# A four-layer convolution kernel: the order of work in the offset stage, the index arithmetic in halves, layer 1's projection by quarters

## The reference

```
om = conv3x3(x, offset_w) + offset_b            # 27 values per position: 18 offsets, 9 masks
dy, dx, mask = om[0:18:2], om[1:18:2], sigmoid(om[18:27])
py, px = row + tap_row + dy, column + tap_column + dx
y0, x0 = floor(py), floor(px);  ly, lx = py - y0, px - x0
val = bilinear(x at (y0, x0), (y0, x0+1), (y0+1, x0), (y0+1, x0+1); ly, lx) * mask
out = relu(batch_norm(einsum(val, weight) + bias))
```

## Time and profile before

| | |
|---|---|
| median of 3 runs | 4148.88 us (4147.64 to 4153.2) |
| profiled execution | 4145.01 us, its span 4143.2 us |
| mean granted clock of TensorE | 0.905 of full |
| busy share of the span | PE 82%, DVE 78%, POOL 54%, PEld 52%, ACT 48% |
| offset stages start (first L838 of the last group norm) | 795.0, 1760.9, 3692.9 us in samples 0, 1 and 3 |

### The profile page before, as it was taken

The page is one execution under the profiler, slowest core; times in us unless marked ns, Lnnn a source line. Parts: engine busy times, 40 slices in busy tenths (PEclk is TensorE's granted clock), DMA queues, the critical chain, the costliest instruction groups (busy, mean ns, idle before and its releaser), DMA issues.

```text
span 4143.2 us, 79222 instructions
## 1 busy us (share of the span) xinstructions
PE 3416.2 (82%) x28785; PEld 2163.6 (52%) x28785; DVE 3239.3 (78%) x6687; ACT 1972.0 (48%) x4413; POOL 2234.6 (54%) x2476
## 2 busy tenths in 40 slices
PE   4999868879999966979999976979999976982555
PEld 2666623447777732336777742435777752342444
DVE  5999767489999856669999956749999966745666
ACT  2444332446666622346666742345666653242333
POOL 3454450068878641038878824018887845005775
PEclk9999989989999988979999988989999998995555
DMA  1000101155555402055555512045555520117775
GB/s 49 9 12 12 42 7 44 60 165 148 154 151 156 120 19 49 14 160 154 150 151 151 153 40 48 2 127 143 156 152 152 151 80 22 39 46 213 219 220 176
DMA packets 219934, 426.57 MB, mean 103 GB/s; under 512 B 27825, under 2 KB 126540, under 8 KB 217512
## 3 DMA queue, kind: packets, MB, share of 16 engines
q0 software_dynamic: 92160, 302.06, 25.3%
q1 hardware_dynamic: 127346, 119.53, 10.0%
q10 hardware_dynamic: 54, 0.01, 0.0%
HBM read 340.77 MB, written 60.65 MB: 97 GB/s over the span
## 4 chain that ended last, share of the span: by engine, by line
PE 37%; DVE 29%; issue 12%; POOL 10%; POOLq 4%; DVEq 3%; ACT 2%; SPq 2%; DMA 1%; ACTq 0%
DVE val L1233 9%; PE bank L548 7%; DVE mxc L1196 7%; PE bank L688 6%; DVE xl L1256 5%; POOL G L1595 3%; DVE val L1243 3%; PE bank L732 3%; PE bank L716 2%; POOLq L1570 2%; PE bank L749 2%; PE bank L475 2%; POOL reg L1595 1%; POOL x_cur L1595 1%; PE bank L571 1%
## 5 line engine op out<-in xcount | busy, mean ns | idle before, releaser
L1606 POOL TENSOR_TENSOR xl<-pt 128x192 bf16<-128x192 f32 (+1 forms) x1024 | 685.5, 670 | 422.6 <-PE bank L548 206.4
L868 ACT ACTIVATE pt<-bank 128x512 f32<-128x512 f32 x1024 | 608.2, 594 | 573.9 <-PE bank L517 343.0
L1595 POOL DMA_INDIRECT G<-patch_table,idx x576 | 593.9, 1031 | 191.9 <-issue 115.1
L548 PEld LDWEIGHTS bank<-vt,pt 128*128 128x128 bf16 x8192 | 548.5, 98 | 242.1 <-ACT pt L868 3.9
L548 PE MATMUL bank<-vt,pt 128*128 128x129 bf16 (+1 forms) x8192 | 632.7, 220 | 1.1 <-ACT osb L876 1.1
L1196 DVE TENSOR_REDUCE mxc<-bank 128x1 f32<-128x512 f32 x896 | 607.1, 679 | 29.0 <-PE bank L475 27.3
L1256 DVE TENSOR_TENSOR xl<-pt 128x320 bf16<-128x320 f32 (+1 forms) x1024 | 504.2, 493 | 72.8 <-PE bank L548 53.7
L548 PE MATMUL bank<-vt,xl 128*128 128x129 bf16 x4096 | 401.2, 221 | 12.8 <-DVE xl L1256 12.7
L1580 POOL TENSOR_TENSOR rs<-ve,mhalf 128x4 f32<-128x4 f32 x32 | 34.9, 1092 | 619.6 <-ACT ve L995 619.6
L475 PE MATMUL bank<-reg,qh 128*128 128x512 bf16 x896 | 341.4, 382 | 13.6 <-DVE mxc L1196 10.1
L688 PE MATMUL bank<-reg,val 128*32 128x512 bf16 x3264 | 271.4, 395 | 66.4 <-DMA G<-xl 66.4
(11 more groups left out here) (249 smaller groups left out, 6906.2 us busy)
## 6 DMA issues: line engine op xcount, KB each, us to landing
patch_table<-valt SPq DMA_DIRECT2D x64, 512.0 KB, 6.6
G<-patch_table,idx POOLq DMA_INDIRECT x576
x_cur<-in_x SPq DMA_DIRECT2D x4, 2048.0 KB, 8.1
xl<-in_x SPq DMA_DIRECT2D x32, 256.0 KB
attn_out<-ob SPq DMA_DIRECT2D x32, 256.0 KB
x_store<-x_cur SPq DMA_DIRECT2D x4, 2048.0 KB, 6.5
xr<-x_store SPq DMA_DIRECT2D x32, 256.0 KB
out<-fo SPq DMA_DIRECT2D x32, 256.0 KB
```

The source lines that it names most:

```text
L548: last = mm(O[t // 2][:, c0:c0 + width], image[:, at % ring, t * 128:(t + 1) * 128], vhl[:, values, st, 0:width], start=(st == 0 and part ...
L868: A(pt[:, at % PT_RING, :], ST[at % ST_RING] if n else ST_FIRST[at % 3], ACT.Exp, scale=SCALE).then_inc(s["exp_done"], 1)
L1595: g.indirect_dma_start(out=patches(j, k), out_offset=None, in_=table[:], in_offset=bass.IndirectOffsetOnAxis(ap=idx[:, j * K1 + k:j * K1 + ...
L1606: g.tensor_tensor(pl[:, at % PL_RING, 0:stop], pt[:, at % PT_RING, 0:stop], ph[:, at % PT_RING, 0:stop], ALU.subtract).then_inc(s["pl_p"], 1)
```

## The change

- `layer3_prepare` on PE: the transposes (`turn`) of chunks 0 to 3 come before the first convolution, and `turn(c + 4)` comes behind `convolve(c)`; the folding matmuls are a function of their own, `by_position`.
- The copy of the normalized chunk to `xst` moves from ACT to POOL, released by each quarter of the image.
- DVE's `indices` is split into `build_grid` (once, in sample 0, kept in a bfloat16 tile `grid`), `coordinates(n, half)` (both axes together) and `index_and_weights(n, half)`. Half 0 (tiles 0 to 15) is done within the offset stage, half 1 after the next sample's group norm. `om_rdy`, `em_rdy` and `idx_rdy` count halves; POOL waits for the second half before the gathers of the third tile.
- The next sample's chunk statistics are taken on DVE behind the last two copies of the offset stage.
- POOL makes the grid's steps in sample 0 alone, and drains at the end of each attention.
- PE's projection in layer 1 waits for the quarter of each chunk.

```diff
         idx = sb("idx", [128, T * K1], U32)
...
-                    wait_alone(sp, s["idx_rdy"], n)
+                    wait_alone(sp, s["idx_rdy"], 2 * n)
...
-                wait_alone(pe, s["gn_xn"], 4 * (4 * n + 2))
                 for c in range(NCH):
+                    wait_alone(pe, s["gn_xn"], 4 * (4 * n + 1) + c // 2 + 1)
...
@@ -758,6 +761,9 @@
                         last = nc.tensor.transpose(TR[u][:, t * 128:(t + 1) * 128],
                                                    xst[:, u, t * 128:(t + 1) * 128], ident[:])
                     last.then_inc(s["xt_ps"], 1)
+
+                def by_position(c):
+                    u = c % 2
                     pe.wait_ge(s["oc_ev"], NCH * n + c + 1 + 2)
                     pe.wait_ge(s["ot_ev"], NCH * n + c + 1)
                     for t in range(TB):
@@ -765,12 +771,16 @@
                                   fold[:], start=True, stop=True)
                     last.then_inc(s["ot_ps"], 1)
 
+                for c in range(4):
+                    turn(c)
                 for c in range(NCH):
                     wait_alone(pe, s["xl_rdy"], 8 * n + 4 + min(c // 2 + 2, 4))
                     convolve(c)
                     if c:
-                        turn(c - 1)
-                turn(NCH - 1)
+                        by_position(c - 1)
+                    if c + 4 < NCH:
+                        turn(c + 4)
+                by_position(NCH - 1)
...
-                with act.Fori(0, NCH // 2) as j:
-                    for u in range(2):
-                        c = j * 2 + u
-                        act.wait_ge(s["xt_ps"], NCH * n + c + 1)
-                        A(as_rows(xst[:, u, :]), rows(c), ACT.Copy).then_inc(s["xs_rdy"], 1)
-                        act.wait_ge(s["oc_ps"], NCH * n + c + 1)
-                        act.wait_ge(s["ot_ps"], NCH * n + c + 1)
-                        A(om54[:, u, :], ST[u][:], ACT.Identity, bias=offb2[:]).then_inc(s["oc_ev"], 1)
-                act.wait_ge(s["om_rdy"], n + 1)
-                A(wrk[6], om[:, :, 18:27], ACT.Exp, scale=-1.0).then_inc(s["em_rdy"], 1)
+                def mask_exponent(half):
+                    tiles = slice(half * HALF, (half + 1) * HALF)
+                    act.wait_ge(s["om_rdy"], 2 * n + half + 1)
+                    A(mask[:, tiles, :], om[:, tiles, 18:27], ACT.Exp, scale=-1.0).then_inc(s["em_rdy"], 1)
+
+                for c in range(NCH):
+                    u = c % 2
+                    act.wait_ge(s["oc_ps"], NCH * n + c + 1)
+                    act.wait_ge(s["ot_ps"], NCH * n + c + 1)
+                    A(om54[:, u, :], ST[u][:], ACT.Identity, bias=offb2[:]).then_inc(s["oc_ev"], 1)
+                    if c == 5:
+                        mask_exponent(0)
+                mask_exponent(1)
...
-            def layer3_prepare(n):
-                low_part(2 * n + 1, range(4))
-                with dve.Fori(0, NCH // 2) as j:
-                    for u in range(2):
-                        c = j * 2 + u
-                        dve.wait_ge(s["xt_ps"], NCH * n + c + 1 + 2)
-                        if not_first(n):
-                            dve.wait_ge(s["conv_ps"], T * n)
-                        v.tensor_copy(cols(xt, c), TR[u][:]).then_inc(s["xt_ev"], 1)
-                        dve.wait_ge(s["ot_ps"], NCH * n + c + 1 + 2)
-                        v.tensor_copy(cols(regq, c, TB * NOFF), MX[u][:, 0:TB * NOFF]).then_inc(s["ot_ev"], 1)
-                dve.drain()
-                dve.sem_inc(s["om_rdy"], 1)
...
+            def layer3_prepare(n, more):
+                def turned(c):
+                    dve.wait_ge(s["xt_ps"], NCH * n + c + 1 + 2)
+                    if not_first(n):
+                        dve.wait_ge(s["conv_ps"], T * n)
+                    v.tensor_copy(cols(xt, c), TR[c % 2][:]).then_inc(s["xt_ev"], 1)
+
+                low_part(2 * n + 1, (0, 1))
+                turned(0)
+                turned(1)
+                low_part(2 * n + 1, (2,))
+                turned(2)
+                turned(3)
+                low_part(2 * n + 1, (3,))
+                for c in range(NCH):
+                    dve.wait_ge(s["ot_ps"], NCH * n + c + 1 + 2)
+                    v.tensor_copy(cols(regq, c, TB * NOFF), MX[c % 2][:, 0:TB * NOFF]).then_inc(s["ot_ev"], 1)
+                    if c % 4 == 3:
+                        dve.drain()
+                        dve.sem_inc(s["om_rdy"], 1)
+                    if c + 4 < NCH:
+                        turned(c + 4)
+                    if c == 3:
+                        coordinates(n, 0)
+                    if c == 5:
+                        index_and_weights(n, 0)
+                    if more and c >= 6:
+                        dve.wait_ge(s["x_in"], 16 * (n + 2))
+                        for q in range(4 * (c - 6), 4 * (c - 5)):
+                            chunk_stats(q)
+
+            def build_grid():
+
+                dve.wait_ge(s["grid_rdy"], 1)
...
+                    v.tensor_copy(grid[:, :, axis::2], (floor if axis else point)[:, :, 0:K1].bitcast(I32))
+                dve.drain()
+                for axis in range(2):
+                    v.tensor_scalar(grid[:, :, axis::2], grid[:, :, axis::2], xcol[:, 1 + axis:2 + axis], None, ALU.add)
+                dve.drain()
+
+            def coordinates(n, half):
+
+                tiles = slice(half * HALF, (half + 1) * HALF)
+                p, fl, up = point[:, tiles, :], floor[:, tiles, :], rest[:, tiles, :]
+                if n == 0 and half == 0:
+                    build_grid()
+                v.tensor_tensor(p, grid[:, tiles, :], om[:, tiles, 0:2 * K1], ALU.add)
+                dve.drain()
+                v.tensor_scalar(p, p, -1.0, float(H), ALU.max, ALU.min)
+                dve.drain()
+                v.tensor_copy(up.bitcast(I32), p)
+                dve.drain()
+                v.tensor_copy(fl, up.bitcast(I32))
+                dve.drain()
+                v.tensor_tensor(up, fl, p, ALU.is_gt)
+                dve.drain()
+                v.tensor_tensor(fl, fl, up, ALU.subtract)
+                dve.drain()
+                v.tensor_tensor(p, p, fl, ALU.subtract)
+                dve.drain()
+                v.tensor_scalar(up, p, -1.0, 1.0, ALU.mult, ALU.add)
+
+            def index_and_weights(n, half):
+
+                tiles = slice(half * HALF, (half + 1) * HALF)
+                (ly, lx), (y0, x0), (hy, hx) = [(a[:, tiles, 0::2], a[:, tiles, 1::2]) for a in (point, floor, rest)]
+                em = mask[:, tiles, :]
                 dve.drain()
                 v.scalar_tensor_tensor(y0, y0, float(TW), x0, ALU.mult, ALU.add)
-                dve.wait_ge(s["em_rdy"], n + 1)
-                v.tensor_scalar(wrk[6], wrk[6], 1.0, None, ALU.add)
-                dve.drain()
-                v.reciprocal(wrk[6], wrk[6])
-                v.tensor_scalar(idx[:].rearrange("p (t k) -> p t k", k=K1), y0, float(TW + 1), None, ALU.add)
-                dve.drain()
-                v.tensor_tensor(hy, hy, wrk[6], ALU.mult)
-                v.tensor_tensor(ly, ly, wrk[6], ALU.mult)
+                dve.wait_ge(s["em_rdy"], 2 * n + half + 1)
+                v.tensor_scalar(em, em, 1.0, None, ALU.add)
+                dve.drain()
+                v.reciprocal(em, em)
+                v.tensor_scalar(idx[:].rearrange("p (t k) -> p t k", k=K1)[:, tiles, :], y0, float(TW + 1), None, ALU.add)
+                dve.drain()
+                v.tensor_tensor(hy, hy, em, ALU.mult)
+                v.tensor_tensor(ly, ly, em, ALU.mult)
                 dve.drain()
                 for corner, (a, b) in enumerate(((hy, hx), (hy, lx), (ly, hx), (ly, lx))):
-                    v.tensor_tensor(w4[:, :, corner * K1:(corner + 1) * K1], a, b, ALU.mult)
+                    v.tensor_tensor(w4[:, tiles, corner * K1:(corner + 1) * K1], a, b, ALU.mult)
                 dve.drain()
...
-            def sample(n, dcn):
-                wait_alone(dve, s["x_in"], 16 * (n + 1))
-                for c in range(NCH):
-                    chunk_stats(c)
+            def sample(n, dcn, more):
+                if not dcn:
+                    dve.wait_ge(s["x_in"], 16)
+                    for c in range(NCH):
+                        chunk_stats(c)
...
-                    indices(n - 1)
+                    coordinates(n - 1, 1)
+                    index_and_weights(n - 1, 1)
...
-                wait_alone(pool, s["xa"], NCH * (n + 1) + 2)
-                g.iota(wrk[9].bitcast(I32), pattern=[[2, T], [1, 3], [0, 3]], base=-1, channel_multiplier=0)
-                g.iota(wrk[10].bitcast(I32), pattern=[[0, T], [0, 3], [1, 3]], base=-1, channel_multiplier=0)
+                for c in range(NCH):
+                    wait_alone(pool, s["gn_xn"], 4 * (4 * n + 3) + c // 2 + 1)
+                    pool.wait_ge(s["xt_ps"], NCH * n + c + 1)
+                    g.tensor_copy(as_rows(xst[:, c % 2, :]), rows(c)).then_inc(s["xs_rdy"], 1)
+
+            def grid_steps():
+
```

(13 more changed lines are left out.)

## The result

The kernel after takes 4087.0 us (median of 4 runs, 4083.0 to 4091.8), against 4148.3 for the kernel before beside it: a ratio of 0.9851, 95% interval 0.9836 to 0.9867. The sign is right, the size is short by almost a half.

A forecast was written before the change was run, and what follows sets the result against it. No single engine was taken as the limit; each stage was read for the wait that ends last. Layer 1 11.2, junctions 9.1 and tail 13.0 sum to 33.3, giving 4115.6 us against the median 4148.88, range 4102 to 4132.

The forecast's parts named there:

- Moved queues, at nothing: SP's waits, POOL's drain at the attention's end and its iotas: no cost; drain at most 1.16 us if uncovered.
- Layer 1 by quarters: Start of layer 1: PE projects after each chunk's quarter, 2.8 us in each of four samples, 11.2; bounds 2.0 and 3.5.
- The tail: Last sample's offset stage: table writes start earlier, the last lands at 3739.9 against 3752.9, 13.0 us; bounds 11 and 14.5.
- The junctions: Between samples: earlier first maxima and faster key chunks, less a later aggregate, 3.5 + 3.5 + 2.1 = 9.1 us.
- statistics inside buy nothing: Offset stage, DVE: what the statistics hide is paid by half 0 and the later convolution; aggregate +0.7, with the port +1.3.
- POOL's copies at 0.65: Offset stage: each f32 copy moved from ACT to POOL takes 0.65 us; even at 1.16 no cost.
- Ports: Offset stage: POOL's copies and DVE's low parts hold each other up, 3.1 us more at three junctions, 4127.5; chance 0.20.
- Clock early: First convolution at 2.4 GHz from the start: 2.0 x 3, and 1.5 at the tail, 4108.1; chance 0.14.
- Junctions nothing: Between samples: the key loop, not DVE, sets the maxima, so nothing is gained there, 4124.7; chance 0.10.
- layer 1 half: Start of layer 1: half the gain, as ACT's restart eats the rest, 4121.2; chance 0.05.
- no change: Table gets no earlier start, held by something else on SP; each junction loses 1 us, 4140.7; chance 0.04.
- copies far dearer: Offset stage: POOL's copy far dearer, slower overall from 3.8 us each; at 4.5, 4171.6; chance 0.03.

The follow-up runs named there:

- b_drain: The kernel before with one edit, POOL draining at the end of each attention: 4119.8 us, ratio 0.9939 to 4147.2.
- a_nodrain: The kernel after without POOL's drain at the attention's end: 4113.3 us, ratio 0.9914.
- b_quarters: The kernel before with one edit, PE's layer 1 projections waiting for the quarter of their chunk: 4131.5 us, ratio 0.9964.
- a_stats_out: The kernel after with the next sample's eight statistics behind the whole offset stage, as in the kernel before: 4089.8 us, ratio 0.9867.
- a_index_out: The kernel after with both halves of index arithmetic behind the next group norm, the last sample keeping half 0 in its stage: 4100.1 us, ratio 0.9893.
- a_ahead2: The kernel after with statistics behind the copies of chunks 2 and 3, and two turns, not four, before the first convolution in samples 0 to 2: 4069.2 us.
- a_mid_two: The kernel after with two drains, behind the 144th and 216th gathers in samples 1 to 3, replacing the one at the attention's end: 4111.5 us.
- a_last: The kernel after with the drain behind the last of 288 gathers in samples 1 to 3, not at the attention's end: 4113.7 us.

## Why the prediction was wrong, step by step

**The step that failed** is "Moved queues, at nothing": "The drain at the attention's end sits on POOL, which has nothing to do until the statistics of the next image; if that cover were gone it would cost the rest of one subtraction, at most 1.16." The cover is there (17.28 us), but a drain behind 288 gathers costs 9.0, not the rest of one subtraction, and the kernel before paid that price at layer 1's first drain, on the path, in samples 1 to 3. I looked at what the added drain would cost and took a drain's price from an engine that had no gathers behind it. I did not look for the next drain behind it in the same queue, nor at the idle time of POOL's groups, where L1571 has 26.9 us. Shown by `b_drain` and `a_nodrain`, from both sides: 27 and 26 us. With 3 x 8.98 = 26.9 in the sum the forecast would have been 4088.7. That the other terms came so near in total (33.9 in `a_nodrain`, interval 30 to 41, against 33.3) is partly luck: the two parts of the junction term were both too large and offset each other, as below.

**Layer 1 by quarters**, 11.2 forecast: 12.1 by the stretches, 9.5 to 20.7 by `b_quarters`. ACT did evacuate chunk 0 as soon as its quarters were done. Right, the size 0.2 a sample low.

**The tail**, 13.0 forecast: 12.8. Copy 7 began 26.1 us behind ACT's first quarter (27.5 forecast), the last write landed 45.8 behind it (47.0). Right in size. Of the two bounds, 0.3 apart in the forecast, it was the other that held: SP had issued the first eight writes by 3673.76 and waited 2.35 us for copy 7, so the second half was bound by that copy and not by the start of the first.

**The junctions**, 9.1 forecast: 7.8 by the stretches (9.7 in the attentions less 1.9 in the stages). The first maximum came 3.6, 4.0 and 3.4 us nearer to the aggregate in samples 1 to 3 (3.6 forecast); DVE was free 12.0 behind the aggregate in sample 2, as computed; ACT's wait of 6.10 for the late key chunk was 1.24, and the granted clock 1.00 where it was 0.50 (its 2.4 and 1.2 GHz levels). Two sizes were wrong. The attentions behind a junction are 3.1, 4.0 and 2.8 shorter, no more than the maxima alone give, so the further 1.2 each for the key chunks out of the lower clock did not show: 9.9 for the 14.4 forecast. And the stages are longer by 0.9, 0.7 and 0.4, where 2.7 (with the grid), 1.3 and 1.3 were counted: 1.9 for 5.3. The difference of the two came out near the forecast by their offsetting. That the statistics inside buy nothing was right at the place where they stand (`a_stats_out`); that they would pay if moved to where DVE waits, I had not seen.

**POOL's copies at 0.65**: 0.62. **The rivals.** Ports: the low parts stretched in sample 0 alone, by 0.4 each for two of them, where 3.1 a stage was at stake; so it happened and cost next to nothing. The mechanism shows more elsewhere: the four products of half a weight set take 0.96 with POOL idle and 2.77 beside POOL's key casts and subtractions, and in `a_index_out` a cast of 0.31 took 1.24 there (rows of DVE above). The Trainium skill (SBUF — State Buffer, "Who interferes with whom") has two-input operations and, in their two-port modes, copies and casts of Vector exclude GpSimd's reads. By that rule both stretch, and the trace agrees. Clock early: partly true and worth little. From its first row to its last the first convolution took 3.40 us in every sample before, at 0.61 a matmul throughout, and 2.62, 2.49, 2.47 and 2.36 after: 3.7 us in all, where the rival had 7.5. Junctions nothing, layer 1 half, no change, and copies far dearer are excluded by the numbers above.

## What to carry to other kernels

The chain of a page can hold a wait without naming it: three waits of 9 us stood under "issue", and the entry that named the drain's line was other time. Look in the groups of each engine for idle time ended by "issue" that a group's neighbours don't have (26.9 us at L1571, 0.0 at L1569), and then at the timeline there; here one line of code removed it. When a change adds or moves a wait, ask for each engine what the same kind of wait costs further down its queue, and whether the new one pays a debt there. And when work is moved into a stage, what counts is which wait it falls into: the same eight statistics bought nothing that the intervals can tell behind the last copies (4087.0 against 4089.8) and 14 us (4087.0 - 4072.9) behind those of the third and fourth chunk.

## What the chip showed that I had not expected

- A `drain` on POOL behind indirect DMAs takes several microseconds, even 73 us after their data were last read: 9.0 behind 288 gathers, 3.1 behind 216, 4.6 behind 144, 6.0 behind 72; with no gather since the last drain, nothing. From 72 to 216 it falls with the count, at 288 it is highest. In an idle stretch of POOL of 17 us it is hidden.
- A POOL copy of 128x512 from f32 to f32 takes 0.62 us, the same as its cast to bf16 (0.61); started while a two-input operation ran on DVE it took 0.82 to 0.84.
- In samples 1 and 2 of `a_ahead2` the first convolution starts after a wait of 2 us and runs at the lower clock throughout (0.61 a matmul). Right behind eight transposes it turned to the higher one 1.2 to 2.5 us later in most stages, but not in sample 0 of `a_stats_out`, `a_mid_two` and `a_last`: there it stayed at 0.61 for all its 3.40 us, and the stage took 46.3 us where that of the kernel after took 45.1. What decides between the two is open.
